# Attention in a fused MoE–attention–MoE kernel: one output bank, four score banks, a written-out TensorE order, and the maxima split on GpSimd

## What is computed

```python
c_q = x @ W_dq
Q = (c_q @ W_uq).reshape(Bx, Sx, N_HEADS, D_K)
...
scores = jnp.einsum('bqhd,bkhd->bhqk', Q, K) / math.sqrt(D_K)
causal = jnp.tril(jnp.ones((Sx, Sx), dtype=bool))
scores = jnp.where(causal, scores, -jnp.inf)
attn = jax.nn.softmax(scores, axis=-1)
out = jnp.einsum('bhqk,bkhd->bqhd', attn, V).reshape(Bx, Sx, N_HEADS * D_K)
```

## Time and profile before

| | |
|---|---|
| Time, median of 3 runs | 1255.79 us (1250.74 to 1257.35) |
| Profiled execution, span of the trace | 1263.3 us |
| TensorE busy in the span | 1066.7 us, 84% |
| VectorE, ScalarE, GpSimd busy | 829.9, 666.1, 384.3 us |
| Attention, first exponential to last output copy | about 425 to 920 us |

### The profile page before, as it was taken

The page is one execution under the profiler, slowest core; times in us unless marked ns, Lnnn a source line. Parts: engine busy times, 40 slices in busy tenths (PEclk is TensorE's granted clock), DMA queues, the critical chain, the costliest instruction groups (busy, mean ns, idle before and its releaser), DMA issues. The chain is left out here.

```text
span 1263.3 us, 22520 instructions
## 1 busy us (share of the span) xinstructions
PE 1066.7 (84%) x6988; PEld 642.3 (51%) x6988; DVE 829.9 (66%) x2536; ACT 666.1 (53%) x1668; POOL 384.3 (30%) x404
## 2 busy tenths in 40 slices
PE   3539999984988899999999999999859369999940
PEld 2328888872442244443444444444347258888840
DVE  6774444436867888888888888888037754444427
ACT  5605554542753376676777666667636315455520
POOL 6506777752002000000000000000048227777730
PEclk8559999995977699999999999999889759999985
DMA  9503333326756444444444444440057113333339
GB/s 301 186 9 93 101 105 105 102 84 216 201 200 142 59 60 61 61 61 60 61 61 60 60 61 61 61 60 11 10 189 239 58 38 94 104 102 104 105 118 331
DMA packets 109248, 132.53 MB, mean 105 GB/s; under 512 B 29968, under 2 KB 83664, under 8 KB 109136
## 3 DMA queue, kind: packets, MB, share of 16 engines
q1 hardware_dynamic: 91280, 89.65, 31.2%
q0 software_dynamic: 13632, 37.24, 9.3%
q10 hardware_dynamic: 4224, 4.19, 1.0%
HBM read 82.42 MB, written 48.23 MB: 103 GB/s over the span
## 5 line engine op out<-in xcount | busy, mean ns | idle before, releaser
L1415 ACT ACTIVATE stacks_rows_or_prob<-stacks_bank 128x512 f32<-128x512 f32 (+3 forms) x768 | 326.0, 494 | 144.1 <-PE stacks_bank L1347 118.9
L1429 DVE CUSTOM_DVE_ANT_0 stacks_bank<-stacks_bank,all_causal 128x128 f32<-128x128 f32 (+3 forms) x512 | 245.4, 504 | 33.7 <-PE stacks_bank L1318 30.2
L1432 DVE TENSOR_REDUCE t_maxp<-stacks_bank 128x1 f32<-128x512 f32 x256 | 175.5, 686 | 25.0 <-PE stacks_bank L1318 24.4
L1318 PE MATMUL stacks_bank<-stacks_kst,stacks_qst 96*128 96x512 bf16 (+2 forms) x528 | 160.3, 348 | 8.5 <-DVE t_maxp L1429 4.2
L1358 PE MATMUL stacks_bank<-stacks_rows_or_prob,stacks_turned_or_values 128*32 128x512 f32 (+3 forms) x1536 | 164.5, 500 | 3.0 <-ACT stacks_rows_or_prob L1415 1.1
L1344 PE MATMUL stacks_bank<-stacks_qst,stacks_kst 99*128 99x512 bf16 (+3 forms) x528 | 154.9, 335 | 2.5 <-ACT stacks_rows_or_prob L1415 1.9
L1296 POOL COPY stacks_turned_or_values<-stacks_values 128x512 f32<-128x512 f32 x16 | 9.8, 613 | 427.7 <-DMA stacks_kst<-qk_parts 286.5
L1318 PEld LDWEIGHTS stacks_bank<-stacks_kst,stacks_qst 96*128 96x128 bf16 x528 | 48.5, 98 | 126.9 <-DVE t_maxp L1429 66.6
L653 PE MATMUL be_psG<-b_w,be_xT 128*128 x426 | 112.8, 401 | 0.0
L653 PE MATMUL ae_psG<-a_w,ae_xT 128*128 x426 | 111.9, 398 | 0.0
L1347 PE MATMUL stacks_bank<-all_causal_t,all_ident_bf 128*128 128x128 bf16 x512 | 109.6, 221 | 0.0
(11 more groups left out here) (296 smaller groups left out, 1917.7 us busy)
## 6 DMA issues: line engine op xcount, KB each, us to landing
stacks_qst<-qk_parts SPq DMA_DIRECT2D x66, 128.0 KB, 4.9
stacks_kst<-qk_parts SPq DMA_DIRECT2D x66, 128.0 KB, 7.6
stacks_rows_or_prob<-y_rows SPq DMA_DIRECT2D x16, 512.0 KB, 6.1
s_yk<-y_rows SPq DMA_DIRECT2D x16, 512.0 KB, 9.4
stacks_parts_or_stacks<-qk_parts SPq DMA_DIRECT2D x60, 128.0 KB, 6.2
qk_parts<-stacks_parts_or_stacks SPq DMA_DIRECT2D x16, 384.0 KB, 2.6
qk_parts<-q_parts SPq DMA_DIRECT2D x16, 384.0 KB, 3.4
o_rows<-t_orow SPq DMA_DIRECT2D x32, 136.0 KB, 8.7
```

Of the source, the lines that this page charges most:

```text
L1318: nc.tensor.matmul(psR[bank][:, 0:w], qst[slot][0:KROWS, h, i * P:(i + 1) * P], kst[slot][0:KROWS, h, k0:k0 + w], start=True, stop=True).t ...
L1415: nc.scalar.activation(prob[j % 2][:, h, a:(c + 1) * 512], psS[n % ST_BANKS][:, a - c * 512:512], ACT.Exp, scale=DK ** -0.5).then_inc(exp_ ...
L1429: ins = nc.vector.tensor_tensor_reduce(psR[bank][:, 0:w], psR[bank][:, 0:w], T.causal[:, 512 - w:512], 1.0, -BIG, ALU.add, ALU.max, maxp[: ...
L1432: ins = nc.vector.tensor_reduce(maxp[:, h, col:col + 1], psR[bank][:, 0:w], AX_X, ALU.max)
```

## The change

Six things change together.

- `psR` gets a fourth bank, and `psO` keeps one. Both output halves now pass through the same bank one after the other, so a p of half 1 must wait for ScalarE's copy of half 0, and the next step's half 0 for the copy of half 1.
- The p (and t) items are therefore ordered half by half: (0..3, c=0), then (0..7, c=1).
- The exponentials of a unit go to one of four slots in turn (`PROBS`), in place of two slots by j and two by half. The room is the same.
- `plan_step` no longer plays the step; it reads the order from a string for each kind of step (`ORDER`): r is any item of the ring (scores, m, o), t a turned score, p a value unit.
- The split of the negated maxima moves from VectorE to GpSimd (`split`), which also takes its copy of the values (`spread`) in a new order around it. VectorE keeps the negation alone.
- TensorE waits for the maxima's DMAs at the first t of a step, no longer at its head; and the fourth early score waits for the last latents, whose bank it now shares.

```diff
-RING_BANKS = 3
+RING_BANKS = 4
 ST_BANKS = 3
+PROBS = 4
...
+ORDER = {
+    (2, True): "rtrtrtrrtrtrtrtrrtrtprttrrrttrtptrtrtrrttrrtpprttrrrtrtrtprtrtrrtrtrtpprtrtrtrrtrtrtprtrrtrttptrtrtrtrtrtrttppp",
...
+def value_units():
+
+    return [(j, c) for c in range(2) for j in range(QT // 2 * (c + 1))]
...
+    pv = [("pv", j, c) for j, c in value_units()]
+    st = [("st", j, c, h) for j, c in value_units() for h in range(HG)]
+    nexts = {"r": iter(ring), "t": iter(st), "p": iter(pv)}
+    order = [next(nexts[what]) for what in ORDER[later, with_before]]
...
-    psR, psS, psO = A.banks[0:3], A.banks[3:6], A.banks[6:8]
+    psR, psS, psO = A.banks[0:RING_BANKS], A.banks[RING_BANKS:RING_BANKS + ST_BANKS], A.banks[RING_BANKS + ST_BANKS]
...
+        def split(g):
+            pool.wait_ge(drained, neg_at(g))
+            wait(pool, m_loaded, g * (16 * PARTS))
+            first.link(nc.gpsimd.tensor_copy(mparts[:, 0], neg[:]))
+            first.link(nc.gpsimd.tensor_tensor(mid[:], neg[:], mparts[:, 0], ALU.subtract))
+            first.link(nc.gpsimd.tensor_copy(mparts[:, 1], mid[:]))
+            nc.gpsimd.tensor_tensor(mparts[:, 2], mid[:], mparts[:, 1], ALU.subtract).then_inc(m_ready, 1)
+            pool.wait_ge(m_ready, g + 1)
...
+            if n == 0:
+                pe.wait_ge(m_loaded, g * (16 * PARTS) + 16 * PARTS)
...
             if j == 0:
-                wait(pe, o_copied, g * 2 + c - 1)
+                wait(pe, o_copied, g * 2 + c)
...
-                if j > 1:
-                    act.wait_ge(pv_done, g * PV + n_pv[j - 2, c] + 1)
-                else:
-                    wait(act, pv_done, (g - 1) * PV + n_pv[j + QHALF * (c + 1) - 2, c] + 1)
+                wait(act, pv_done, g * PV + n + 1 - PROBS)
...
+                    if m + 1 in turned:
+                        copy_out(g, turned.index(m + 1))
...
-            dve.wait_ge(drained, r + 1)
-            link(nc.vector.tensor_copy(mparts[:, 0], neg[:]), g, 2)
-            link(nc.vector.tensor_tensor(mid[:], neg[:], mparts[:, 0], ALU.subtract), g, 3)
-            link(nc.vector.tensor_copy(mparts[:, 1], mid[:]), g, 4)
-            nc.vector.tensor_tensor(mparts[:, 2], mid[:], mparts[:, 1], ALU.subtract).then_inc(m_ready, 1)
```

More of the change, by code:

```diff
@@ L1132, in plan_step @@
     if with_before:
-        at = 4 if later else 0
+        at = OUT_AT if later else 0
         ring[at:at] = [("o", c) for c in range(2)]
[L1135 to L1177, removed]
-        else:
[L1179 to L1183, removed]
@@ L1184, in plan_step @@
-    return order, [x for x in order if x[0] in "smo"]
+    pv = [("pv", j, c) for j, c in value_units()]
+    st = [("st", j, c, h) for j, c in value_units() for h in range(HG)]
+    nexts = {"r": iter(ring), "t": iter(st), "p": iter(pv)}
+    order = [next(nexts[what]) for what in ORDER[later, with_before]]
+    assert len(order) == len(ring) + len(st) + len(pv)
+    turned = [sum(x[0] == "st" for x in order[:order.index(("pv", QT // 2 * (c + 1) - 1, c))]) for c in range(2)]
+    return order, ring, turned
@@ L1198, in programs_attention @@
     MROW = HG * QT
[L1199 removed]
+    n_pv = {(j, c): n for n, (j, c) in enumerate(value_units())}
     n_st = {(j, c, h): n * HG + h for (j, c), n in n_pv.items() for h in range(HG)}
@@ L1287, in early_ones, with neg_at, spread @@
             Q.pool_chain.link(nc.gpsimd.memset(kst[s][KROWS:MROWS, :, :], 1.0))
+    def neg_at(g):
+        if g == 0:
+            return NS + 1
+        return ring_base(g - 1) + plans[min(2, NG - g), g > 1][1].index(("m", 1)) + 1
     def gpsimd(pool):
         first = Q.pool_chain
-        def step(g, k, later, with_before):
-            wait(pool, loaded[k], ((g - k) // SLOTS) * (16 * N_LOADS) + 16 * N_LOADS)
+        def split(g):
[6 more added lines that the diff above has]
+            pool.wait_ge(m_ready, g + 1)
+        def spread(g):
+            k = g % SLOTS
+            pool.wait_ge(loaded[k], (g // SLOTS) * (16 * N_LOADS) + 16 * N_LOADS)
             b, hg = g // A.GB, g % A.GB
             rows = A.values[:, bass.ds(b * QT, QT), bass.ds(hg * (HG * DK), HG * DK)]
[L1296 to L1303, removed]
-                first.link(nc.gpsimd.memset(kst[SLOTS - 1][KROWS:MROWS, :, :], 1.0))
+            nc.gpsimd.tensor_copy(vst[k][:].rearrange("p j (h w) -> p j h w", w=VW)[:, :, :, 0:DK],
+                                  rows.rearrange("p j (h w) -> p j h w", w=DK)).then_inc(spread_done, 1)
+            pool.wait_ge(spread_done, g + 1)
         def blank(s):
@@ L1310, in gpsimd @@
         pool.wait_ge(Q.c_done, Q.CH)
-        blank(0)
+        for s in range(SLOTS):
+            blank(s)
         pool.wait_ge(Q.v_ready, Q.CH)
-        steps(step)(pool)
+        split(0)
+        spread(0)
+        pool.wait_ge(Q.v_ready, 2 * Q.CH)
+        for stored in Q.parts_stored:
+            pool.wait_ge(stored, (Q.CH // 2) * (16 * Q.NU))
+        first.link(nc.gpsimd.memset(kst[SLOTS - 1][KROWS:MROWS, :, :], 1.0))
+        spread(1)
+        spread(2)
+        for g in range(NG - 1):
+            split(g + 1)
+            if g + SLOTS < NG:
+                spread(g + SLOTS)
     def score(pe, u, slot, r, bank):
```

48 lines of the change are left out of this document (24 added, 24 removed).

## The result

The changed kernel takes 1216.59 us in the median of four runs (1209.06 to 1221.96), before 1255.79: the ratio is 0.968, with a 95% interval of [0.963, 0.973]. One more run of before, of 3489.65 us, counts as slow and stands in neither the median nor the ratio. The forecast was 1231 us with a range down to 1219; the changed kernel is faster than both. Its profiled execution has a span of 1212.9 us, where before's had 1263.3.

A forecast was written before the change was run, and what follows sets the result against it. TensorE's own stream was taken to bound the step. A steady step saves 0.7 and 0.8 us, 20 us over 13 steps; plus 1.4 and 3.4 makes 25 us off the 1255.8 median: 1231 us, range 1219 to 1247.

The forecast's parts named there:

- the term of the waits: Steady attention step: TensorE loses some 1.6 us to waits, VectorE causing about 1.0 and ScalarE 0.6; 0.8 saved.
- I let 0.2 of the 1.0 us remain: Steady step, TensorE's waits for VectorE's maxima: fourth bank and split off VectorE leave 0.2 of 1.0 us; bounds 0 and 1.0.
- I leave the 0.6 us as it is: Steady step, TensorE's waits for ScalarE: order by halves, one output bank and four slots leave 0.6 us; bounds 0.1 and 1.6.
- All waits go: Rival for the steady steps: another 0.8 us a step saved, 10 us in all, giving 1220 us; chance 0.12.
- The budget of 14 us of TensorE against 14 of VectorE for 28 ring items: First third of the new steady string, its densest stretch: VectorE can follow TensorE with four banks of lead.
- the busy time of 26.1: Steady step without the split on VectorE: VectorE needs about 26.1 of some 29 us, 0.5 us per r on average.
- Places of p: Steady step on TensorE: 8 places instead of 12 save four switches into and out of p, 0.18 us each.
- all of 0.72: Upper bound, and the value taken, for the steady step's saving from fewer switches into p: 0.72 us; lower bound nothing.
- First step, last but one, last: Attention steps outside the 13 steady ones: savings of 1.4, 0 and 3.4 us from fewer switches and waits.
- the spare 0.8 us: Split on GpSimd between m and the next step's first t: 2.3 us available, 1.5 needed, so hidden.
- a possible 0.3 us of t: Steady step, ScalarE copying half 0 between fourth and fifth p: with three t banks the last two t may wait 0.3 us.

The follow-up runs named there:

- products apart: Changed kernel with each pp and ppp of the steady step's order broken up, 12 places of p instead of 8: steady step 29.52 us, whole run 1228.9 us.
- GpSimd late: Changed kernel with the split's second GpSimd instruction done four times, so the parts come 1.48 us later: 0.98 us added to the steady step, whole run 1245.8 us.
- only the split moved: Kernel before with the split of the negated maxima moved to GpSimd and nothing else: steady step 30.81 us, whole run 1258.0 us.
- the kernel with the earlier m: Changed kernel with another order in the last step but one, its maxima and m some 4 us earlier: two last steps 59.02 us instead of 63.32, run 1216.0 us.

## Why the prediction was wrong in size

The direction, and the mechanism of fewer places and fewer waits in TensorE's stream, were right. The step that failed is the term of the waits: 0.8 us a step were taken off, and 1.47 went.

- **Waits, the failing term.** The text put the waits of before at some 1.6 us a step by counting the stream, and 1.47 is what was there. But it took only 0.8 of it off: "I let 0.2 of the 1.0 us remain" for VectorE, and for ScalarE "I leave the 0.6 us as it is". All 1.47 went: 0.67 x 13 = 8.7 us. The rival "All waits go", 1220 us with a chance of 0.12, was the case. The shares themselves, 1.0 for VectorE and 0.6 for ScalarE, came from sums of waits that mostly ran under streaming matmuls; by the starts they are 0.7 and 0.7.
- **The reason given for it.** The fourth bank and the split off VectorE stood as one item. In this order the split is worth 0.00 us of a steady step and the bank 2.90. The budget of 14 us of TensorE against 14 of VectorE for 28 ring items compared sums over a third of the step, and so did the busy time of 26.1: adding 0.75 us to VectorE changed nothing, while one bank less cost four times that. What decides is how far TensorE may run ahead through the densest few r. And leaving ScalarE's share as it was overlooked that the string also sets where t stands: with the fourth bank, the order takes away 1.10 us of waits, at t and p alone.
- **Places of p.** 0.18 us was taken, 0.23 measured: 0.05 x 4 x 13 = 2.6 us. The upper bound, all of 0.72, lay below the 0.92 that came; the exit is 0.12, and a p behind a p also has a shorter first pass. The rule of the Trainium skill that was weighed there (TensorEngine Tiling (Array Packing), Tiling Modes, Key Properties: a change of mode drains, a change of tile does not) agrees with the saving; the products apart show it at 0.92 of their 1.19 us.
- **Steps that were not steady.** The sum took every step behind the first at the steady gain. In before's execution 3.8 us lay in steps longer than the steady one, in after's 0.4. Two of the three long ones stood where a part of the maxima landed late and the step's head waited. What makes a landing late wasn't tried. The versions in which the parts come too late for a steady step had more of it (GpSimd late 6.4 us over 13 steps, only the split moved 6.8). Four more kernels with the changed order of the steady step, four banks and the parts in time had 0.2 to 0.8, so the small figure repeats; of before there is one execution.
- **First step, last but one, last.** 2.8, 0.75 and 2.8 us against 1.4, 0 and 3.4. The idle time before the last step was forecast at 4.2 and is 4.3.
- **GpSimd.** Forecast 1.5 us, measured 1.65, hidden as forecast; of the spare 0.8 us, 0.5 to 0.57 are there. The three gaps between its operations took 0.07 to 0.08 us each, not 0.1. The Trainium skill (GPSIMD Engine Reference, Engine selection) speaks for VectorE here: about twice as slow on GpSimd for two inputs, near line rate for one. The same operations on 32x128 took 285 and 419 ns on GpSimd and 215 and 280 ns on VectorE in the kernel with the split back, 1.3 and 1.5 times: a smaller gap for two inputs and a larger one for one than the page has. By that rule the move costs, and it does where no work hides it: with the split back on VectorE the last step took 31.5 us instead of 32.1.
- **One output bank.** Costed at nothing beyond a possible 0.3 us of t. With three maxima banks the second output bank changed the step by less than 0.01 us; with four it has no room, but there no p starts beyond its normal distance.

The sum: 31.2 + 3.5 + 2.8 + 0.75 + 2.8 = 41.0 us, where 25 was forecast.

## What to carry to other kernels

Banks of a ring and the order of the work that fills them are one design: here the written order alone moved the step from 30.92 us by +0.3, the bank with a newly planned order by -0.6, bank and written order together by -2.6, of which 0.92 are the merged p. Busy sums over a step can't say whether a ring waits; look at the densest few items and count the banks of lead. And where one engine's stream is the bound, ask what of its waits *can* stay when the stream is laid out anew, not what share of them the old order gave to whom.

## What the hardware showed unasked

A p behind a p is shorter not only at the seam, where the way out of the p ahead took 409, 303 and 196 ns by its starts (512, 384 and 256 columns) instead of 525, 418 and 312: its own first pass took 409, 196 and 90 ns (512, 256 and 128 columns) instead of 433, 220 and 114. The 4.3 us of idle time ahead of the last step was followed by 3.3 us at the 1.2 GHz level, as this window of the changed kernel shows, where the kernel with the earlier m stayed at 2.4 GHz through its last two steps; the last step itself, from its negation on, got only 0.45 us shorter, since it now holds more of the work behind m (256 matmuls where there were 210), and its t still wait for exponentials.

```profile
841.90:845.20 3.30, 3.30 (x16) 2.24 (x15) 0.44 (x1) 2.17 (x5) 0.00 (x0) 0.50 0.00 0
```
